# Reading two PSUM banks per exponential and per maximum in a four-block transformer kernel

## The reference

```python
scores = jnp.einsum('bhqd,bhkd->bhqk', q, k)
probs = jax.nn.softmax(scores, axis=-1)
o = jnp.einsum('bhqk,bhkd->bhqd', probs, v)
x = x + gate1 * (o @ proj_w + proj_b)
x = x + gate2 * (gelu(norm(x) @ fc1_w + fc1_b) @ fc2_w + fc2_b)
```

## Time and profile before

| | us |
|---|---|
| median of 3 runs | 1167.29 (1166.8 to 1167.61) |
| the profiled execution's own time | 1168.58 |
| its span, first to last instruction | 1166.8 |
| PE busy | 1097.9 (94%) |
| ACT busy | 807.1 (69%) |
| DVE busy | 706.4 (61%) |
| POOL busy | 491.8 (42%) |

### The profile page before, as it was taken

One profiled execution on the slowest core, in us unless ns is written; L12 is line 12 of the kernel. 1 busy time (PEld: TensorE's weight loads), 2 busy tenths in 40 slices (PEclk: granted clock), 3 DMA queues, 4 the chain that ended last, 5 costly groups with the idle time before them and its releaser, 6 DMA issues.

```text
span 1166.8 us, 19882 instructions
## 1 busy us (share of the span) xinstructions
PE 1097.9 (94%) x6717; PEld 703.1 (60%) x6717; DVE 706.4 (61%) x1484; ACT 807.1 (69%) x1439; POOL 491.8 (42%) x447
## 2 busy tenths in 40 slices
PE   8799999889899999999999999999999999999985
PEld 6576877655664665656656657666656566545432
DVE  7454547535165265234775865865865865898874
ACT  3563655478787778897587686687687686676763
POOL 3452642523633625444334553354344344344232
PEclk9999999999999999999999999999999999999998
DMA  6000000313313203321122231122131121131301
GB/s 233 17 29 18 11 10 12 76 42 101 87 29 82 65 1 82 83 64 28 28 74 74 69 82 29 28 74 65 29 90 29 38 56 51 48 90 45 93 9 39
DMA packets 36387, 64.47 MB, mean 55 GB/s; under 512 B 7208, under 2 KB 22312, under 8 KB 36288
## 3 DMA queue, kind: packets, MB, share of 16 engines
q1 hardware_dynamic: 36288, 63.20, 20.4%
HBM read 22.90 MB, written 2.12 MB: 21 GB/s over the span
## 4 chain that ended last, share of the span: by engine, by line
PE 67%; ACT 11%; DVE 11%; issue 5%; POOL 4%; DMA 1%; ACTq 0%; SPq 0%; POOLq 0%; DVEq 0%
PE AVB L698 12%; PE ring L586 12%; PE ring L587 10%; PE ring L588 10%; PE ring L685 10%; PE ring L660 5%; ACT probs L876 4%; DVE m L1184 3%; PE ring L629 2%; ACT gT_h L942 2%; PE ring L718 1%; ACT gT_f L942 1%; ACT L876 1%; DVE stats L1042 1%; PE ring L723 1%
## 5 line engine op out<-in xcount | busy, mean ns | idle before, releaser
L876 ACT ACTIVATE probs<-ring 128x512 f32<-128x512 f32 x768 | 400.2, 618 | 125.8 <-PE ring L660 77.4
L1184 DVE TENSOR_REDUCE m<-ring 128x1 fp32r<-128x512 f32 x512 | 319.9, 682 | 109.8 <-PE ring L660 78.8
L685 PE MATMUL ring<-SQ,SK 64*128 64x512 f32 x768 | 238.9, 439 | 12.7 <-ACT probs L876 5.2
L660 PE MATMUL ring<-SK,SQ 63*128 63x512 f32 x512 | 197.8, 457 | 7.6 <-ACT probs L876 5.8
L685 PEld LDWEIGHTS ring<-SQ,SK 64*128 64x128 f32 x768 | 109.9, 185 | 146.8 <-issue 50.9
L698 PE MATMUL AVB<-probs,V 128*32 128x512 f32 x1536 | 195.3, 614 | 0.1
L1287 POOL TENSOR_TENSOR gT_l<-gT_f,gT_h 128x512 fp32r<-128x512 f32 x96 | 121.0, 1282 | 81.7 <-ACT gT_h L942 79.7
L586 PE MATMUL ring<-w_h,gT_h 128*128 128x256 f32 x384 | 110.4, 288 | 2.5 <-ACT gT_h L942 1.3
L660 PEld LDWEIGHTS ring<-SK,SQ 63*128 63x128 f32 x512 | 84.5, 184 | 39.5 <-ACT probs L876 31.2
L587 PE MATMUL ring<-w_l,gT_h 128*128 128x256 f32 x384 | 106.7, 278 | 0.0
L588 PE MATMUL ring<-w_h,gT_l 128*128 128x256 f32 x384 | 106.6, 278 | 0.0
(11 more groups left out here) (183 smaller groups left out, 2114.8 us busy)
## 6 DMA issues: line engine op xcount, KB each, us to landing
SQ<-qh SPq DMA_DIRECT2D x96, 128.0 KB, 2.6
SK<-kh SPq DMA_DIRECT2D x96, 128.0 KB, 2.8
SQ<-ql SPq DMA_DIRECT2D x48, 128.0 KB, 2.7
SK<-kl SPq DMA_DIRECT2D x48, 128.0 KB, 2.8
raw<-in_w SPq DMA_DIRECT2D x20, 256.0 KB, 2.8
wmod_s<-in_wmod SPq DMA_DIRECT2D x6, 512.0 KB, 3.9
gates<-gate_rows SPq DMA_DIRECT2D x12, 256.0 KB, 3.6
raw<-in_wqkv SPq DMA_DIRECT2D x9, 256.0 KB, 2.8
```

Source lines behind the costliest of these rows:

```text
L660: mm = pe.matmul(o[:, :], SQ[a % 4][r:r + KS, n // 2, c * P:(c + 1) * P], SK[a % 4][r:r + KS, n // 2, :], start=True, stop=True)
L685: mm = pe.matmul(o[:, :], SK[a % 4][r:r + KS + 1, n // 2, c * P:(c + 1) * P], SQ[a % 4][r:r + KS + 1, n // 2, :], start=True, stop=True)
L876: act.activation(probs[:, n % PROBS, :], bank(kind, a, i)[:, :], ACT.Exp, scale=SCALE[layer(unit_job(a))]).then_inc(done["scores"], 1)
L1184: nc.vector.tensor_reduce(m16[:, 80 * (a % 2) + col:80 * (a % 2) + col + 1], bank(kind, a, i)[:, :], AX_X, ALU.max, negate=True).then_inc( ...
```

## The change

The ring becomes one PSUM tensor of seven banks, so that one instruction can address two of them. Where two scores of a unit (an even one and the next) take neighbouring banks that don't wrap around the ring's end, ACT waits for the second product, does one exponential over both banks (1024 columns) into two neighbouring slots of `probs`, and then releases both. The same holds for maxima on DVE: one reduction over two banks into two columns of `m16`, eight apart. `row_pairs` now lists two scores, two maxima, two scores, two maxima. The due times of most tables and the patterns are altered; `START` puts a load of the first feed-forward weights first.

```diff
-    if not maxima:
-        return scores
-    return [s for n in (0, 2) for s in (scores[n], maxima[n + 1], scores[n + 1], maxima[n])]
+    return scores[:2] + maxima[:2] + scores[2:] + maxima[2:]
...
-        ring = [ctx.enter_context(nc.psum_tensor(f"ring{i}", [P, TOK], F32)) for i in range(RING)]
+        rings = ctx.enter_context(nc.psum_tensor("rings", [P, RING * TOK], F32))
+        ring = [rings[:, TOK * i:TOK * i + TOK] for i in range(RING)]
+
+        def double(kind, a, i):
+
+            first = USE[(kind, a, i - i % 2)]
+            return USE[(kind, a, i - i % 2 + 1)] == first + 1 and first % RING < RING - 1
+
+        def two_banks(kind, a, i):
+            first = USE[(kind, a, i)] % RING
+            return rings[:, TOK * first:TOK * first + 2 * TOK].rearrange("p (n k) -> p n k", n=2)
...
-                elif kind == "scores":
-                    n = nth("scores", a, i) - 1
-                    act.wait_ge(pe_ring, use(kind, a, i))
+                elif kind == "scores" and not (double(kind, a, i) and i % 2):
+                    n, two = nth("scores", a, i) - 1, double(kind, a, i)
+                    act.wait_ge(pe_ring, use(kind, a, i + two))
...
-                    act.activation(probs[:, n % PROBS, :], bank(kind, a, i)[:, :], ACT.Exp,
-                                   scale=SCALE[layer(unit_job(a))]).then_inc(done["scores"], 1)
+                    if two:
+                        act.activation(probs[:, n % PROBS:n % PROBS + 2, :], two_banks(kind, a, i), ACT.Exp,
+                                       scale=SCALE[layer(unit_job(a))]).then_inc(done["scores"], 2)
+                    else:
+                        act.activation(probs[:, n % PROBS, :], bank(kind, a, i)[:, :], ACT.Exp,
+                                       scale=SCALE[layer(unit_job(a))]).then_inc(done["scores"], 1)
...
-                elif kind == "max":
-                    n, c = i % 4, i // 4
-                    col = ((n % 2) * 2 + n // 2) * TT + c
-                    dve.wait_ge(pe_ring, use(kind, a, i))
+                elif kind == "max" and not (double(kind, a, i) and i % 2):
+                    n, c, two = i % 4, i // 4, double(kind, a, i)
+                    col = 80 * (a % 2) + ((n % 2) * 2 + n // 2) * TT + c
+                    dve.wait_ge(pe_ring, use(kind, a, i + two))
...
+                    if two:
+                        nc.vector.tensor_reduce(m16[:, col:col + 9:8], two_banks(kind, a, i), AX_X, ALU.max,
+                                                negate=True).then_inc(done["max"], 2)
+                    else:
+                        nc.vector.tensor_reduce(m16[:, col:col + 1], bank(kind, a, i)[:, :], AX_X, ALU.max,
+                                                negate=True).then_inc(done["max"], 1)
```

Of the tables, three for example, the patterns of layer 2 (and others), a table of due times, and the start:

```diff
-PAIR = ("p6 A p6 0 p4 1", "p6 A p6 0 p4 1", "p8 A p2 0 p6 1", "p6 A p6 0 p6 1", "p6 A p8 0 p4 1", "p6 A p6 0 p6 1", "p6 A p6 0 p4 1", "p6 A p6 0 p4 1")
+PAIR = ("p6 A p8 0 p6 1", "p6 A p6 0 p4 1", "p8 A p2 0 p8 1", "p6 A p6 0 p6 1", "p6 A p8 0 p4 1", "p6 A p8 0 p6 1", "p6 A p8 0 p6 1", "p6 A p8 0 p4 1")
...
-QKV = {"hT1": (-19.2, -14.24), "q": (-12.95, -10.6), "k": (-12.7, -10.05), "v": (-8.75, -5.05),
-       "stack": (-8.25, -7.35, -2.05, 0.75), "stat1": (-22.15,), "norm1": (-21.3,)}
+QKV = {"hT1": (-18.7, -14.34), "q": (-12.95, -10.7), "k": (-13.3, -10.65), "v": (-8.75, -5.35),
+       "stack": (-8.25, -7.85, -2.25, 0.45), "stat1": (-22.35,), "norm1": (-20.25,)}
...
-START = [("stat1", 0, 0), ("load_mod", 0, 0), ("load_qkv", 0, 0), ("load_qkv", 0, 2), ("load_mod", 0, 1),
-         ("load_w1", 0, 0), ("load_w1", 0, 2), ("load_qkv", 0, 1), ("split_qkv", 0, 0), ("load_wp", 0, 0),
+START = [("load_w1", 0, 0), ("stat1", 0, 0), ("load_mod", 0, 0), ("load_qkv", 0, 0), ("load_qkv", 0, 2),
+         ("load_mod", 0, 1), ("load_qkv", 0, 1), ("load_w1", 0, 2), ("split_qkv", 0, 0), ("load_wp", 0, 0),
```

More of the change, by code:

```diff
@@ L59, in direct @@
     return layer(j) in (0, LAYERS - 1)
-SINGLE0 = {"stat1": (-15.75,), "norm1": (-20.45,), "hT1": (-14.95, -14.29), "q": (-9.01, -5.16), "k": (-5.75, -4.5),
-           "v": (3.06, 5.72), "scores0": (-0.4, -0.2, 1.76, 3.41), "soft0": (1.76, 2.41, 4.61, 5.17),
+SINGLE0 = {"stat1": (-16.2,), "norm1": (-23.7,), "hT1": (-15.4, -14.74), "q": (-11.01, -9.91), "k": (-5.2, -3.95),
+           "v": (2.61, 5.47), "scores0": (-0.85, -0.65, 1.31, 3.06), "soft0": (1.31, 1.96, 4.26, 4.92),
            "pT0": (6.87, 7.42, 7.68, 9.03), "av0": (10.18, 10.73), "proj": (12.69, 13.94), "stat2": (13.99,),
-           "norm2": (14.84,), "bias": (-2.7,)}
@@ L67 @@
-SINGLE1 = {"stat1": (-21.05,), "norm1": (-10.8,), "hT1": (-11.18, -10.83), "q": (-8.12, -4.31), "k": (-8.57, -7.36),
-           "v": (2.6, 3.92), "scores0": (-1.64, -1.29, 1.78, 1.88), "soft0": (2.49, 2.84, 3.36, 3.71),
-           "pT0": (7.11, 7.47, 7.82, 8.68), "av0": (11.73, 12.09), "proj": (13.16, 13.41), "stat2": (13.72,),
+           "norm2": (14.84,), "bias": (-3.15,)}
+SINGLE1 = {"stat1": (-21.05,), "norm1": (-4.8,), "hT1": (-11.18, -10.83), "q": (-8.12, -4.01), "k": (-8.57, -7.31),
+           "v": (2.6, 3.92), "scores0": (-1.64, -1.29, 1.78, 2.88), "soft0": (2.49, 2.84, 3.36, 3.71),
+           "pT0": (7.11, 7.47, 7.82, 8.68), "av0": (11.73, 12.09), "proj": (13.16, 13.41), "stat2": (13.82,),
@@ L70 @@
            "norm2": (14.33,), "bias": (-5.4,)}
[L71 to L76, removed]
@@ L87 @@
[L87 to L90, removed]
+SINGLE2 = {"stat1": (-16.5,), "norm1": (-14.55,), "hT1": (-9.7, -9.49), "q": (-6.76, -3.06), "k": (-5.65, -3.6),
+           "v": (3.0, 4.07), "scores0": (-0.14, 0.81, 1.78, 4.23), "soft0": (2.59, 4.44, 5.01, 5.51),
+           "pT0": (7.92, 8.38, 8.63, 8.99), "av0": (12.74, 12.9), "proj": (13.98, 14.38), "stat2": (16.24,),
+           "norm2": (16.64,), "bias": (-0.3,)}
@@ new lines @@
+FFN0 = {"hT2": (16.72, 17.27), "fc1": (20.32, 20.68, 21.03, 21.44, 24.73, 25.09, 26.87, 27.22), "gelu": (21.79, 27.58),
+        "fc2a": (24.96, 26.06), "fc2": (30.57, 32.88)}
+FFN2 = {"hT2": (24.6, 24.78), "fc1": (25.63, 25.81, 25.99, 26.17, 30.02, 30.19, 31.09, 31.77), "gelu": (26.55, 31.85),
+        "fc2a": (27.67, 29.21), "fc2": (32.06, 32.32)}
+FIRST = {("v", 0, 0): -4.01, ("v", 0, 1): -2.7, ("modrow", 0, 1): 2.11, ("headscale", 1, 0): -0.84, ("mod", 0, 1): 4.47,
[3 rows of a table added]
+NEXT1 = {("modrow", 1, 0): 16.25, ("mod", 1, 0): 21.0, ("load_mod", 1, 1): 28.0, ("modrow", 1, 1): 30.8,
+         ("mod", 1, 1): 31.6, ("load_gate", 1, 0): 39.25, ("split_qkv", 1, 0): 46.12, ("load_qkv", 1, 1): 42.32,
+         ("split_qkv", 1, 1): 49.36, ("load_qkv", 1, 2): 45.84, ("split_qkv", 1, 2): 50.15, ("load_qkv", 1, 0): 41.9,
+         ("vones", 4, 0): 56.69, ("vones", 5, 0): 67.95}
@@ L91 @@
+LEAD_IN = {"stat1": (-24.09,), "norm1": (-23.23,), "hT1": (-14.74, -14.56), "qktok": (-12.53, -12.04, -11.51, -10.52),
+           "qkss": (-12.22, -11.69, -11.15, -10.36), "qkroot": (-10.28,), "v": (-7.19, -7.01), "qkrs": (-9.94,),
+           "qknorm": (-9.71, -9.63, -9.35, -9.17), "q": (-8.33, -7.97), "k": (-8.15, -7.79),
+           "stack": (-7.03, -6.95, -0.36, 1.0),
            "gmax": (-5.39, -5.21, -5.03, -4.85, -4.67, -4.49, -3.6, -3.42, -2.52, -2.34, -2.16, -1.98, -1.8, -1.62, -1.44, -1.26),
@@ L93 @@
 COSINE = {"hT1": (-15.95, -15.04), "qktok": (-13.9, -13.8, -12.05, -11.4), "qkss": (-12.9, -12.7, -11.9, -10.95),
-          "qkroot": (-10.5,), "v": (-10.95, -9.4), "qkrs": (-9.9,), "qknorm": (-9.8, -9.75, -9.6, -9.55),
-          "q": (-8.9, -8.4), "k": (-8.8, -8.2), "stack": (-7.3, -6.0, -2.65, 0.6), "stat1": (-18.0,), "norm1": (-17.2,),
+          "qkroot": (-10.5,), "v": (-10.95, -9.2), "qkrs": (-10.15,), "qknorm": (-9.85, -9.8, -9.65, -9.6),
+          "q": (-8.9, -8.4), "k": (-8.8, -8.2), "stack": (-7.3, -6.0, -2.35, 0.9), "stat1": (-18.0,), "norm1": (-17.2,),
@@ L101 @@
+ATTN = {"oT1": (17.1, 17.56, 17.57, 17.83), "oT2": (18.45, 18.71), "proj": (19.2, 19.85), "stat2": (20.7,),
         "norm2": (22.55,)}
[L102 removed]
+FFN = {"hT2": (23.5, 23.91), "fc1": (25.7, 25.91, 25.92, 25.93, 29.55, 29.56, 29.57, 29.58), "gelu": (25.94, 29.59),
        "fc2a": (27.45, 29.55), "fc2": (30.55, 31.2)}
[L104 to L105 removed]
@@ L106 @@
[L106 to L114, removed]
@@ L126 @@
-FFN1 = {"hT2": (17.27, 17.77), "fc1": (21.12, 21.48, 21.53, 21.59, 25.29, 25.65, 27.03, 28.08), "gelu": (21.94, 28.39),
-        "fc2a": (26.02, 27.97), "fc2": (34.2, 34.43)}
-START = [("stat1", 0, 0), ("load_mod", 0, 0), ("load_qkv", 0, 0), ("load_qkv", 0, 2), ("load_mod", 0, 1),
-         ("load_w1", 0, 0), ("load_w1", 0, 2), ("load_qkv", 0, 1), ("split_qkv", 0, 0), ("load_wp", 0, 0),
[3 rows of a table removed]
+FFN3 = {"hT2": (23.3, 23.61), "fc1": (25.6, 25.61, 25.72, 25.73, 29.65, 29.66, 29.67, 29.68), "gelu": (25.74, 29.69),
+        "fc2a": (26.65, 27.9), "fc2": (31.15, 31.55)}
@@ new lines @@
+OUTPUT = {"gatefix": (20.05,), "final": (23.3, 25.45, 26.35, 31.45), "store": (27.25, 30.85, 30.95, 33.7),
+          "bias": (18.35,)}
```

(23 more changed lines are left out.)

18 lines of the change are left out of this document (removed), and 12 rows, old and new, of tables (FIRST, START).

## The result

The changed kernel takes 1225.11 us (median of 4 runs, 1217.37 to 1229.67) against 1167.45 for the kernel before in the same runs: slower by 57.7 us, ratio 1.0481, 95% interval 1.0458 to 1.0504. The forecast was 1146.6 us, with a range to 1174. The direction was wrong, and the loss is over four times the +13 us of the slower rival.

The account below looks back on a forecast made before the run. TensorE was taken to be held back by ScalarE and VectorE returning banks; -23 us of savings, +2 for late release and +0.3 for start gave -20.7, so 1146.6 us against a median of 1167.29, range 1124 to 1174.

Parts of the forecast that it names:

- the slower rival: At TensorE's claims of banks held until a pair's second half is read: +13 us, 1180 us; chance 0.18.
- What bounds the kernel: TensorE looks at its limit but is held back by readers of banks, up to 33 us of a layer-2 stretch.
- the order: Two scores then two maxima keeps the 0.23 us start spacing possible on TensorE; costed at nothing.
- the times: Shifted steps could move the 12 jobs by +-14 us if all went one way; taken as 0.
- the wait for the second product: A two-bank instruction waits for its second product, 0.23 us at most when TensorE is free; within the 2 us charge.
- the late release: A pair's first bank returns 0.43 us later on ScalarE, 0.54 on VectorE; charged 2 us, mainly at run ends.
- start: A 256 KB weight load put first delays loads behind it by 1.1 us; taken as 0.3 us.
- The fixed parts: Each paired exponential saves 95 ns, each paired maximum 83 ns: 32 us less ScalarE work, 18 less VectorE work.
- the sum's 23 us: Reader savings on the path: 8 and 1 us in layer 3, 8 in layer 2, 6 in layer 1.
- those 8 for layer 3: Layer 3 is close to VectorE-bound, so nine tenths of 9.0 us saved by 109 paired maxima shorten it.
- the 212 waits: TensorE's weight loads waited 104 us for maxima and exponentials; a third of these waits getting longer would cost 34 us.
- the faster rival: Pairing also mends TensorE, so the 104 us of bank waits fall by a third, 35 us: 1132 us; chance 0.2.

Follow-up runs that it names:

- singles: The changed kernel with every exponential and maximum over one bank again, order of products and due times as changed: 1180.26 us, ratio 1.0095.
- late claims alone: Against single instructions that wait for both products and release singly, TensorE takes a pair's first bank as free only when the second is read: 1228.95 us.

## Why the prediction was wrong

**What bounds the kernel** was read rightly: TensorE is held back by its readers, through the ring. The step that failed followed from it: I took a reader's *work* as the price of a bank. The price is the time for which a bank is away.

Step by step from 1167.45 us, and from kernels measured in different rounds: the order and the times bring 12.8 us (1180.26; 11.3 against the kernel before beside it), the wait for the second product 3.4 (1183.70), the late release 42.2 (1225.91), the two-bank instructions -0.8 (1225.11). In the prediction's sum these stood at 0.3 for all of order, times and start, 2 for the late release with the wait, and -23.

**The fixed parts** (95 ns a pair, a mean over the exponentials as they stood, and 83, from ten maxima in a row) didn't come off in full, since few pairs follow each other without a wait: ScalarE saved 12.7 us of work, below the 19 us of the prediction's lower end, and VectorE 9.8, below its 18. Nor are they seen on the path: two-bank instructions and single ones with the same release differ by 0.8 us (1225.11 and 1225.91). So the sum's 23 us were worth nothing that these runs can show, those 8 for layer 3 too, where "the stretch is as long as VectorE's work plus 6.5 us" looked safe. A queue that keeps a reader busy exists only while banks suffice to keep it filled.

**The late release** was charged 2 us, with the words "in a run this is returned at once, since two banks come free together". It cost 42 us (1183.70 to 1225.91), or 57 in the old order. I had written that two banks with each reader leave three for TensorE where one with each left five, and let it pass. The three are too few. My reading of the piece of layer 3 above is that a pair needs two of them before its reader can start, claims are in order, and the other sort's pair stands in between. The rival named this mechanism and its sign. Its price, 34 us from a third of the 212 waits, came near the 42 measured by luck, for it rests on waits that exist in the kernel before. Its sum, +13 us, fell short of 57.7 mostly because it still took off the 21 us of saving and had nothing for the order. I gave it 0.18. Taking one bank away (31 us) would have shown beforehand that a bank is worth more than the whole saving hoped for.

**The rule on breaking instructions up.** The slower rival's page, the Trainium skill, Perfetto Trace Analysis, section Optimizing Scalar/DVE Operations, held here: breaking work up lets it complete sooner where Scalar and Vector cause bubbles without being saturated. The runs agree (1180.26 us with singles, 1225.11 with pairs), with a limit: instructions that are broken up but give their banks back together gain nothing (1225.91). In the changed kernel the stretch at 89% of VectorE (51.16 of 57.71) lost most, 10.4 us; with the late release alone in the old order it was layer 2 (94.56 for 85.34 us, against 64.10 for 57.71 in layer 3). The section's other advice, to group where the engine is saturated, gave nothing that can be seen.

**A bound in the faster rival** was also misread: the readers' work "falls by 8% at most" goes by the 32 us expected of 400.2; its own upper end of 65 us is 16%.

**The order** was costed at nothing on the ground that both orders alternate between halves of the array. It costs 18.7 us at the old times and 13.6 at the new. That two products of one sort in a row leave the other reader without work is my explanation; no run shows it apart from the order itself. **The times** were within their +-14 us. **Wait for the second product**: 3.4 us, a small cost as thought, and hardly clear of the spread. **The start**: the last copy of the first layer-1 job stands at 323.32 us in the changed kernel and at 318.44 before, but between 316.6 and 323.9 in kernels that share the new start, so no price can be read from it.

**The clock** was in none of my terms. In the layer-3 stretch of the changed kernel TensorE was busy 2.67 of the 4 us from 1128, standing mostly for banks in between; then its clock fell, and the next 10 us passed at a mean of 0.52, almost all at the lower level. Columns as in the earlier trace rows:

```profile
1128.00:1132.00 4.00, 2.67 (x13) 1.29 (x12) 3.76 (x4) 3.48 (x5) 0.00 (x0) 0.93 0.46 123
1132.00:1142.00 10.00, 10.00 (x45) 3.21 (x47) 5.68 (x8) 4.68 (x6) 2.14 (x3) 0.52 0.26 72
```

The four timed runs of the changed kernel had a mean granted clock of 0.974, 0.967, 0.965 and 0.962 and took 1217.37, 1224.14, 1226.08 and 1229.67 us: 1 us for 0.001. Carried on to the 0.982 of before, some 8 us more would go, to about 1209. By this estimate 16 of the 57.7 us come from the lower clock, and the rest from the waits. That is an upper end: a run with longer waits can have both the longer time and the lower clock. Over the 50 runs of the kernel before that stand beside the experiments, the slope is 0.5 us for 0.001, which would make it some 7. No run held the clock fixed, so the share stays open.

## What to carry to other kernels

Before merging two reads of PSUM, count the banks: those with the readers, those that the next instruction needs filled, and those left for the writer. If the producer already waits for banks, an instruction that holds two until its end can cost more than its fixed part saves, as it did here with ScalarE busy for 74% of a layer-2 stretch and VectorE for 89% of a layer-3 one. Price a buffer by taking one away in the kernel as it is, besides counting the waits that its trace already shows; and test the late release alone, which needs no new instruction.

## What was not expected of the hardware

A read across a bank border cost nothing extra: 1028 ns for 1024 columns against 601 for 512 on ScalarE, 1221 against 682 on VectorE, slopes of 0.83 and 1.05 ns a column, the same as within a bank. And where TensorE waited more, with waits for banks of up to 0.9 us, its clock was lower too: with late claims alone, at equal work, a layer-3 stretch is 68.95 us long at 0.89, the next fence, against 59.73 at 1.00 in the fence further up.

```profile
1085.63:1154.58 68.95, 63.86 (x366) 30.86 (x366) 51.88 (x100) 42.52 (x80) 22.94 (x27) 0.89 0.24 58
```
